# xDeepFM on one core: the dense rows turned together with x0's rows, the high halves made later, the sums and the gathers in another order, other pairs spread by TensorE

## What is computed

```
emb = tables[field, sparse]                     # 2048 x 26 x 32
linear = lin_sparse_w[field, sparse].sum(-1) + dense @ lin_dense_w
xk = emb
for w, b in ((conv1_w, conv1_b), (conv2_w, conv2_b)):      # the two layers on products
    hp = einsum('bhd,bmd->bhmd', xk, emb)       # 26*26, then 64*26 rows
    xn = sigmoid(einsum('oi,bid->bod', w, hp) + b)          # 128 rows
    xk, kept = xn[:, :64], xn[:, 64:]
cin = concat(kept).sum(-1) @ cin_w + cin_b
h1 = tanh(deep_x @ W1 + b1); h2 = tanh(h1 @ W2 + b2); h3 = tanh(h2 @ W3 + b3)   # 845-1024-512-256
out = linear + cin + h3 @ deep_w + deep_b + bias
```

## Time and profile before

| | us |
|---|---|
| median of 3 runs | 1764.49 |
| their range | 1760.94 to 1777.09 |
| the profiled execution | 1765.62 |
| its span | 1763.8 |
| PE busy in it | 1603.8 (91%) |
| DVE busy | 1103.3 (63%) |
| ACT busy | 702.8 (40%) |
| POOL busy | 748.4 (42%) |

### The profile page before, as it was taken

The page is one execution under the profiler, slowest core; times in us unless marked ns, Lnnn a source line. Parts: engine busy times, 40 slices in busy tenths (PEclk is TensorE's granted clock), DMA queues, the critical chain, the costliest instruction groups (busy, mean ns, idle before and its releaser), DMA issues.

```text
span 1763.8 us, 23496 instructions
## 1 busy us (share of the span) xinstructions
PE 1603.8 (91%) x6840; PEld 691.1 (39%) x6840; DVE 1103.3 (63%) x992; ACT 702.8 (40%) x981; POOL 748.4 (42%) x631
## 2 busy tenths in 40 slices
PE   0799899989898989798989998989898997999998
PEld 0333333323333333233333333323333333877886
DVE  2277677767676767476767875757676776434432
ACT  1444344334343434343434434334343342445443
POOL 6628273728282826373737372637364111000000
PEclk9899999999999999899999999989999999999999
DMA  4678687968697868587878886867687773233231
GB/s 88 127 181 195 158 192 175 201 151 190 162 188 164 188 160 191 139 180 171 182 165 179 192 190 158 183 154 183 164 184 163 188 185 102 90 97 97 88 101 48
DMA packets 111802, 277.59 MB, mean 157 GB/s; under 512 B 26035, under 2 KB 46803, under 8 KB 111703
## 3 DMA queue, kind: packets, MB, share of 16 engines
q1 hardware_dynamic: 98456, 270.11, 63.4%
q0 software_dynamic: 13312, 7.06, 4.2%
HBM read 270.03 MB, written 7.04 MB: 157 GB/s over the span
## 4 chain that ended last, share of the span: by engine, by line
PE 51%; POOL 26%; issue 11%; DMA 5%; ACT 4%; DVE 2%; POOLq 0%; ACTq 0%; DVEq 0%
POOL emb L438 22%; PE y L631 20%; PE bc L745 15%; PE xn L625 12%; DMA emb<-table,idx_stage 5%; PE bc L611 2%; POOL r L453 2%; PE bc L618 1%; POOL r L456 1%; ACT halves L785 1%; PE bc L594 1%; PE bc L603 1%; DVE xb L549 1%; DVE hp L549 1%; ACT r L807 1%
## 5 line engine op out<-in xcount | busy, mean ns | idle before, releaser
L549 DVE TENSOR_TENSOR hp<-bc,xk 128x1024 f32<-128x1024 f32 x384 | 452.7, 1216 | 426.0 <-PE bc L611 426.0
L438 POOL DMA_INDIRECT emb<-table,idx_stage x416 | 504.8, 1213 | 147.0 <-issue 133.2
L549 DVE TENSOR_TENSOR xb<-xb,xk 128x1024 f32<-128x1024 f32 x448 | 547.3, 1266 | 26.2 <-ACT xk L806 25.5
L625 PE MATMUL xn<-sq,w1s 128*128 128x512 f32 x768 | 392.3, 650 | 78.2 <-ACT r L807 74.9
L631 PE MATMUL y<-xb,w2s 128*64 128x512 f32 x1792 | 432.7, 596 | 0.7 <-ACT r L811 0.4
L631 PE MATMUL y<-hp,w2s 128*64 128x512 f32 x1536 | 382.6, 605 | 0.1
L453 POOL TENSOR_TENSOR r<-r 128x512 f32<-128x512 f32 x96 | 123.6, 1294 | 444.0 <-ACT r L811 320.1
L801 ACT ACTIVATE sq<-bc 128x1024 f32<-128x1024 f32 x192 | 182.9, 1026 | 271.4 <-PE bc L618 265.9
L625 PEld LDWEIGHTS xn<-sq,w1s 128*128 128x128 f32 x768 | 146.6, 205 | 272.6 <-issue 140.9
L805 ACT ACTIVATE xk<-xn,bias 64x512 f32<-64x512 f32 x128 | 87.1, 680 | 325.5 <-PE xn L625 323.3
L631 PEld LDWEIGHTS y<-xb,w2s 128*64 128x64 f32 x1792 | 122.1, 137 | 238.4 <-issue 203.5
(11 more groups left out here) (63 smaller groups left out, 1028.4 us busy)
## 6 DMA issues: line engine op xcount, KB each, us to landing
xb<-x_rows SPq DMA_DIRECT2D x896, 256.0 KB, 4.8
w_raw<-W SPq DMA_DIRECT2D x32, 448.0 KB, 3.3
w_raw<-W SPq DMA_DIRECT2D x16, 512.0 KB, 3.3
emb<-table,idx_stage POOLq DMA_INDIRECT x416
x_rows<-deep_t SPq DMA_DIRECT2D x16, 384.0 KB
w_raw<-W SPq DMA_DIRECT2D x8, 256.0 KB, 2.5
hp<-select SPq DMA_DIRECT2D x2, 512.0 KB, 4.8
x_rows<-deep_t SPq DMA_DIRECT2D x16, 45.0 KB
```

The source lines that it names most:

```text
L438: nc.gpsimd.indirect_dma_start(out=emb[:, m, :], out_offset=None, in_=table, in_offset=bass.IndirectOffsetOnAxis(ap=idx_stage[:, m:m + 1], ...
L549: nc.vector.tensor_tensor(product(n)[:, :], x[:, :], xk[sl % 2][:, :], ALU.mult).then_inc(multiplied, 1)
L625: last = nc.tensor.matmul(xn[:, :], w1s[:, k, :], sq[k][:, cols], start=(k == 0), stop=(k == K1 - 1))
```

## The change

Five things change together.

- In the tile's third step (`SL_DEEP` = 2) the deep rows are turned right behind x0's rows (`T`, `D0`, `D1`), and no longer at the step's end. ACT copies them there.
- ACT makes the high halves of the next tile after both reads of `xn` in the second step (`sl` = 1), and no longer between `copy_x0` and the first read.
- Pairs 3, 4, 7, 8, 9 and 10 are spread by PE in place of 2, 3, 5, 6, 8 and 9, and the contractions of a step go 0 to 2, 3 and 4, 5 to 8 between the fills, in place of 0 and 1, 2 to 4, 5 to 8. `ORDER` is rearranged to it. The counts of products by PE and by DMA stay six and seven.
- The gathers go in batches of 6, 8, 6 and 6 with sums between, in place of 12, 6, 4 and 4 (`AHEAD`), and the sum of `r1` of step 2 and `make_low` change places with others.
- SP issues `dump` before the spreads of the fourth step (`sl` = 3), and waits for its landing after them (`await_dump`).

```diff
--- before.py
+++ after.py
@@ -42,10 +42,11 @@
 PART = 16
 
 
-ORDER = [3, 10, 0, 7, 4, 1, 8, 11, 2, 9, 5, 12, 6]
-BY_PE = (2, 3, 5, 6, 8, 9)
+ORDER = [3, 10, 4, 0, 7, 11, 5, 1, 8, 2, 9, 12, 6]
+BY_PE = (3, 4, 7, 8, 9, 10)
 assert sorted(ORDER) == list(range(PAIRS))
 BY_DMA = tuple(n for n in range(PAIRS) if n not in BY_PE)
 
 
 
@@ -53,18 +54,17 @@
 STEP_WORK = (
     ("fill", (("K", 0), ("K", 1), ("K", 2))),
     ("of_last", (9, 10, 11, 12)),
-    ("fill", (("T", 0),)),
+    ("fill", (("T", 0), ("D", 0), ("D", 1))),
     ("first", 0),
-    ("fill", (2, 3)),
-    ("of_this", (0, 1)),
+    ("fill", (3, 4)),
+    ("of_this", (0, 1, 2)),
     ("first", 1),
-    ("fill", (5, 6)),
-    ("of_this", (2, 3, 4)),
-    ("fill", (8, 9)),
+    ("fill", (7, 8)),
+    ("of_this", (3, 4)),
+    ("fill", (9, 10)),
     ("of_this", (5, 6, 7, 8)),
 )
 LEFT = STEP_WORK[1][1]
-
 SL_DEEP = 2
 DEEP_PARTS = range(0, 4), range(4, KD)
 SLOTS = 3
@@ -79,8 +79,8 @@
         fills = [use for use in fills if not is_k(use)]
     if ahead == 0 and sl >= STEPS - 2:
         fills = [use for use in fills if not is_t(use)]
-    if sl == SL_DEEP and ahead > 0:
-        fills = fills + [("D", 0), ("D", 1)]
+    if ahead == 0 or sl != SL_DEEP:
+        fills = [use for use in fills if not is_d(use)]
     return fills
 
 
@@ -124,7 +124,7 @@
 
 
 
-AHEAD = 12, 18
+AHEAD = 6, 14, 20
 assert AHEAD[-1] <= M
 
 
@@ -377,6 +377,8 @@
                              deep_t[:, 0:KD - 1, cols]).then_inc(dumped, 16)
                 sp.dma_start(x0_rows[bass.ds(t, 1), (KD - 1) * P:M * ROW, :].rearrange("t p b -> p (t b)"),
                              deep_t[0:LAST_E, KD - 1, cols]).then_inc(dumped, 16)
+
+            def await_dump(t):
                 sp.wait_ge(dumped, t * (16 * DUMPS) + 16 * DUMPS)
                 hold()
 
@@ -389,15 +391,18 @@
             def tile(t, is_first, ahead):
                 for sl in range(STEPS):
                     s = t * STEPS + sl
+                    if sl == SL_DEEP + 1 and ahead > 0:
+                        dump(t + 1)
                     for i, n in enumerate(BY_DMA):
                         if not (is_first and sl == 0):
                             sp.wait_ge(contracted, contracted_by(s - 1, n))
                             hold()
                         spread_by_dma(t, sl, i)
                 if ahead > 0:
-                    dump(t + 1)
+                    await_dump(t + 1)
 
             dump(0)
+            await_dump(0)
             over_tiles(sp, tile)
 
 
@@ -469,27 +474,27 @@
                 stage(t + 1)
 
             free_emb(0, 3)
-            gather(range(AHEAD[1]))
+            gather(range(AHEAD[2]))
 
             def tile(t, is_first, ahead):
-                if ahead > 0:
-                    gather(range(AHEAD[1], M - 4))
                 if not is_first:
                     add_up(t - 1, STEPS - 1, r2, r2_step, y2_read, 1, sum2)
                 if ahead > 0:
-                    gather(range(M - 4, M))
+                    gather(range(AHEAD[2], M))
                 add_up(t, 1, r1, r1_step, xn_read, 2, sum1)
                 if ahead > 0:
                     make_low(t + 1)
+                add_up(t, 2, r1, r1_step, xn_read, 2, sum1)
                 add_up(t, 1, r2, r2_step, y2_read, 1, sum2)
-                add_up(t, 2, r1, r1_step, xn_read, 2, sum1)
-                add_up(t, 3, r1, r1_step, xn_read, 2, sum1)
                 if ahead > 1:
                     free_emb(t + 1, filled_by(t, SL_DEEP, ("D", 1), ahead))
                     gather(range(AHEAD[0]))
+                add_up(t, 3, r1, r1_step, xn_read, 2, sum1)
+                if ahead > 1:
+                    gather(range(AHEAD[0], AHEAD[1]))
                 add_up(t, 2, r2, r2_step, y2_read, 1, sum2)
                 if ahead > 1:
-                    gather(range(AHEAD[0], AHEAD[1]))
+                    gather(range(AHEAD[1], AHEAD[2]))
 
             over_tiles(pool, tile)
             add_up(TILES - 1, STEPS - 1, r2, r2_step, y2_read, 1, sum2)
@@ -692,9 +697,13 @@
                     for kind, what in STEP_WORK:
                         if kind == "fill":
                             uses = [use for use in what if use in there]
+
                             for use in uses:
-                                slot_free(t, sl, use, is_first, ahead)
+                                if is_product(use):
+                                    slot_free(t, sl, use, is_first, ahead)
                             for use in uses:
+                                if not is_product(use):
+                                    slot_free(t, sl, use, is_first, ahead)
                                 fill(t, sl, use, ahead)
                         elif kind == "of_last" and not start:
                             for n in what:
@@ -715,10 +724,6 @@
                         for n in LEFT:
                             pe.wait_ge(multiplied, multiplied_by(s, n))
                             contract(n)
-                    for use in there:
-                        if is_d(use):
-                            slot_free(t, sl, use, is_first, ahead)
-                            fill(t, sl, use, ahead)
 
             over_tiles(pe, tile)
 
@@ -843,8 +848,13 @@
                                 if is_t(use) and use in there:
                                     act.wait_ge(filled, filled_by(t, sl, use, ahead))
                                     copy_x0(slot_of(sl, use, ahead), (sl + 2) % STEPS)
-                                    if sl == 1 and ahead > 0:
-                                        make_high(t + 1)
+                                if is_d(use) and use in there:
+                                    act.wait_ge(filled, filled_by(t, sl, use, ahead))
+                                    if use[1] == 0:
+                                        copy_deep(slot_of(sl, use, ahead), t + 1, DEEP_PARTS[0], 0).then_inc(deep_copied, 1)
+                                    else:
+                                        copy_deep(slot_of(sl, use, ahead), t + 1, DEEP_PARTS[1][:-1], 0)
+                                        copy_deep_last(slot_of(sl, use, ahead), t + 1, KD - 1 - DEEP_PARTS[1][0])
                         elif kind == "of_last" and not start:
                             if sl == 1 and not is_first:
                                 act.wait_ge(r2_step, t * SUMS)
@@ -856,13 +866,8 @@
                                 if sl == STEPS - 1:
                                     act.wait_ge(r1_step, (t + 1) * SUMS)
                             read_xn((sl + 1) % 2, (sl + 1) % STEPS, what)
-                    if ("D", 0) in there:
-                        act.wait_ge(filled, filled_by(t, sl, ("D", 0), ahead))
-                        copy_deep(slot_of(sl, ("D", 0), ahead), t + 1, DEEP_PARTS[0], 0).then_inc(deep_copied, 1)
-                        act.wait_ge(filled, filled_by(t, sl, ("D", 1), ahead))
-                        copy_deep(slot_of(sl, ("D", 1), ahead), t + 1, DEEP_PARTS[1][:-1], 0)
-                        copy_deep_last(slot_of(sl, ("D", 1), ahead), t + 1, KD - 1 - DEEP_PARTS[1][0])
-
+                            if what == 1 and sl == 1 and ahead > 0:
+                                make_high(t + 1)
             over_tiles(act, tile)
 
             def upper_x(g, k):
```

## The result

The kernel after takes 1644.1 us in the median of 4 runs (1642.1 to 1645.5), the kernel before 1762.7. The ratio is 0.935, with a 95% interval of 0.930 to 0.941: faster by 6.5%. The forecast was 1644.

What follows compares the result with a forecast made beforehand. PE bounds every step once its stalls behind the gathers go. Removing stalls gives 114.8 us, the holes 7: 122 off the profiled 1765.6 is 1643.6, median 1.1 lower, stated as 1644, range 1635 to 1680.

Steps and rivals of the forecast that it cites:

- The bound and the loop: PE bounds plain steps; in sl = 1 late gathers stall it about 7 us, recurring because emb is freed late.
- the high halves behind the reads: ACT in sl = 1: making them after xn's second read takes the wait for gathers off xn's path; 12 us slack.
- comes 14 us earlier: POOL's first gather, at 18.4 us of the step before, comes 14 us earlier through the early turning of the deep rows.
- The sum: Tile 0 to tile 15, sl = 1 turnings: 1327.7 us becomes 1212.9 without stalls, 114.8 less; 122 with the holes.
- a small hole: PE ahead of the first layer's half 1: contracting product 2 there saves 0.12 us in 60 steps, 7 us.
- The low halves beside products 11 and 12: POOL's low halves run together with these DVE products: at worst 0.5 us in 14 tiles, 7 us; taken as 0.
- The slots: DVE's products meet PE's needs in the new slot order, the tightest by 0.4 us; cost taken as nothing.
- Rival C: Inner loop: PE waits for products over 0.4 us late; at 1 us late 0.6 us a step, 1680; chance 0.08.
- The gathers in time: Last gather lands 60 us after x0's turning in sl = 2, ACT wants it at 72.3: 12 us of slack.
- rival B: Gathers still too slow, landing at 78 us for 72.3 wanted: stall and half clock cost 60 us, 1705; chance 0.05.
- The dump: SP issues it ahead of sl = 3's spreads: 2 us of transfer first, 12 us for the first spreads to land; cost 0.

Runs made afterwards that it cites:

- b1: The kernel before with one edit, the high halves made behind the second read of xn in sl = 1: 1668.8 us, ratio 0.942.
- a1: The kernel after with the high halves back at their old place, ahead of the reads of xn: 1643.8 us, ratio 0.928.
- a2: The kernel after with the high halves at their old place and POOL's order and batches as before: 1701.2 us, ratio 0.960.

## Why the prediction was right, and where it wasn't

- **The bound and the loop.** Right, and shown: PE's stall was the wait for the gathers, through the high halves and the reads of xn. Moving the need (b1) removes all but 2.3 of its 98.7 us, moving the start (a1) all; with the place of the high halves and POOL's order both old most of it is back (a2). What the prediction didn't see is that the parts don't add up. It summed one effect and was right in that; had it been asked for the worth of each part, "the high halves behind the reads" and "comes 14 us earlier" would have been counted twice.
- **The sum.** 114.8 us expected by removing the stalls, 119.4 measured in the same interval. The deep turning costs 0.79 us, not 0.98, and the steps are 19.94 to 19.96, not 19.97: 0.25 us in 15 deep steps and some hundredths in the others make the 4.6. The prediction's sum has 114.8 + 7 = 121.8 for this interval, 2.4 too much. Ahead of the interval the span is 3.3 us shorter and behind it 0.9, but the 3.3 is no gain of the change. In the profile of the kernel after again the interval begins at 96.39, later than the 95.91 of before, and takes the same 1208.3 us:

```profile
96.39 0.66 PE L599 MATMUL bc<-idr,halves 128*128 128x128 f32 x4
```

That the median fell on the forecast within 0.1 us is luck: the two profiled executions of this kernel took 1642.1 and 1646.1, and the prediction's own sum, 1643.6 less 1.1, gives 1642.5 where it says 1644.

- **The pairs, "a small hole" of 0.12 us, 7 us.** The step that failed. Three contractions ahead of half 1 take 824.02 - 821.29 = 2.73 us, against 3 x 0.885 = 2.66, so some 0.07 of the 0.12 stay with three as well. With the old pairs all the steps outside sl = 1 are 3.8 us longer together, 1.5 of it in one tile: most of the term of 7 us was not there. The deep turning and the shorter steps, 4.6 us, made up for most of what was missing. The new pairs did bring 20 us, by a mechanism that the prediction didn't have (next point).
- **The low halves beside products 11 and 12, 0 taken, 7 at worst.** Nothing was lost in the kernel after, so the value was right, and product 12 was late by less than the bound: it ended at 916.43 - 898.19 = 18.2 in the step, 1.5 us behind the forecast's 16.7 and ahead of the 18.9 where PE wants it (timeline of DVE, where the window holds this product alone):

```profile
914.00 2.43 DVE L554 TENSOR_TENSOR xb<-xb,xk 128x1024 f32<-128x1024 f32 x1
```

What the prediction left out are POOL's two sums behind the low halves. They bring DVE's loss to 9.37 - 5.75 = 3.6 us, 2.1 of it on the next step's products. With product 10 from xb, the low halves and the first of these sums cost 0.87 us a tile, 13 of the 20 us. The prediction looked at this place only for a loss, and it is where the new pairs earn most of what they are worth.

- **The slots, 0.4 us of margin.** Right to a tenth; an added 1.15 us cost 0.74 a step. Rival C was priced by it at 0.6 for 1 us.
- **The gathers in time (rival B).** Landing 12 us early was forecast; 10 us more were absorbed. B didn't come about, and its price wasn't measured.
- **The dump, 0.** No loss, as said; DVE never waits for a spread, the landings took 9.9 us at most (9.0 before), the DMA shares are 0.72 to 0.92. That the early dump could be a gain was left out, and the waits in the run with the late one speak for some 8 us.

## What to carry to other kernels

A stall in a loop of transfers can be cured by asking later or by starting earlier; work out the slack of both in a timetable of one cycle, since here, once one was positive, the other was worth nothing. Freeing a buffer early is worth little while the engine that refills it has something else to wait for first: look at what stands ahead in its order. When all steps are as long as the bounding engine's work, the busy share of the others says little. The worth of an edit depends on what stands beside it: the new pairs brought 20 us beside POOL's new order, while beside the old one the step in question had nothing to gain. What counts is the margin at each hand-over, and operations that collide should be placed where the product behind them isn't wanted next.

## What the runs showed of the hardware

DVE products with both inputs in SBUF and GpSimd's operations on SBUF slow each other down. Without the other a product takes 1.21 us and five in a row, which overlap a little, 5.75, the two operations of the low halves 2.70, a sum 1.29. In the kernel after product 12 takes 2.43, the low halves 3.75 and the sum behind them 2.25. DVE's loss of 3.6 us over five products is about GpSimd's work beside them, the second of the low halves and two sums, 1.35 + 1.29 + 1.29 = 3.9 us when alone. Products that read PSUM keep their time beside low halves, gathers and sums. The Trainium skill ("SBUF — State Buffer", section on the two separate sides) tells of a lock of the shared port for whole instructions, between a DVE operation with two SBUF inputs and a GpSimd operation that reads SBUF. The trace agrees: product 12's 2.43 us are two lengths of 1.21. The low halves and the sums read SBUF, so they meet the condition, which the prediction left unsaid.

The issue of a gather is slowed by such products as well, but hardly slows them. In the kernel after, beside five products from xb it takes up to 1.97 us, and 0.94 when they are done; the five take 5.93 us in place of 5.75 (timelines of DVE and POOL):

```profile
852.69 5.93 DVE L554 TENSOR_TENSOR xb<-xb,xk 128x1024 f32<-128x1024 f32 x5
...
857.47 1.97 POOL L443 DMA_INDIRECT emb<-table,idx_stage  x1 [0.30 <-issue]
859.74 0.94 POOL L443 DMA_INDIRECT emb<-table,idx_stage  x1 [0.30 <-issue]
```

Not every set of runs of this kernel is alike. The kernel before had medians of 1763 to 1773 us in four sets of runs and 1838 in one, on another chip, and in traces taken beside that one engines started late where the trace names no cause, ACT by up to 10.9 us in the run with six more gathers. Whether it is the chip or something else of that time isn't shown.
